# Reordered ends of a one-core attention and feed-forward kernel: queue order of the first transfers, place of the last heads' sum, and products of zeros

## The reference

```
x = x + layernorm(attention(layernorm(x)))          # 8 heads of 64, causal, sinusoidal position added to q and k
x = x + layernorm(tanh(layernorm(x) @ W1 @ W2 @ W3 + bias))
```

## Time and profile before

| | us |
|---|---|
| median of three runs | 561.74 |
| lowest and highest | 560.62 and 562.1 |
| the profiled execution | 561.25 |
| its span | 559.4 |

### The profile page before, as it was taken

The page is one execution under the profiler, slowest core; times in us unless marked ns, Lnnn a source line. Parts: engine busy times, 40 slices in busy tenths (PEclk is TensorE's granted clock), DMA queues, the critical chain, the costliest instruction groups (busy, mean ns, idle before and its releaser), DMA issues.

```text
span 559.4 us, 16795 instructions
## 1 busy us (share of the span) xinstructions
PE 537.3 (96%) x4595; PEld 455.6 (81%) x4595; DVE 469.5 (84%) x2063; ACT 409.4 (73%) x1507; POOL 398.9 (71%) x650
## 2 busy tenths in 40 slices
PE   7799999999999999999999999999999999999971
PEld 4588888888888888888888888888888888888850
DVE  4987898888889888888888888988888888888843
ACT  2777877778778777777877877777787787777740
POOL 3535777877777787777787777778777777776653
PEclk9999999999999999999999999999999999999985
DMA  5000011100000100000100010011000011100000
GB/s 160 29 2 21 11 30 30 30 19 28 20 18 28 28 28 19 28 17 21 28 28 25 22 28 9 28 28 28 19 28 24 14 28 28 28 9 21 21 9 19
DMA packets 27963, 14.53 MB, mean 26 GB/s; under 512 B 1700, under 2 KB 27431, under 8 KB 27943
## 3 DMA queue, kind: packets, MB, share of 16 engines
q1 hardware_dynamic: 27510, 13.51, 8.5%
q10 hardware_dynamic: 432, 0.79, 0.4%
HBM read 10.09 MB, written 4.19 MB: 26 GB/s over the span
## 4 chain that ended last, share of the span: by engine, by line
PE 92%; DVE 3%; ACT 2%; issue 1%; DMA 1%; POOL 1%; POOLq 0%; DVEq 0%; ACTq 0%
PE scores L879 18%; PE turned_and_heads L933 17%; PE misc_bank L994 11%; PE qk_bank L894 6%; PE qk_bank L896 5%; PE qk_bank L895 5%; PE turned_probs L910 5%; PE turned_probs L911 5%; PE turned_and_heads L919 5%; PE misc_bank L865 4%; PE misc_bank L977 3%; PE misc_bank L867 3%; PE misc_bank L866 3%; PE misc_bank L939 2%; PE misc_bank L975 1%
## 5 line engine op out<-in xcount | busy, mean ns | idle before, releaser
L263 ACT ACTIVATE probs<-scores,neg_max 128x256 f32<-128x256 f32 (+1 forms) x512 | 208.6, 425 | 43.4 <-DVE neg_max L631 43.3
L631 DVE CUSTOM_DVE_ANT_0 scores<-scores,mask 128x256 f32<-128x256 f32 (+1 forms) x512 | 166.2, 386 | 11.4 <-PE scores L879 11.4
L641 DVE TENSOR_TENSOR qk<-qk_bank,pe 128x512 f32<-128x512 f32 x128 | 87.4, 683 | 32.9 <-PE qk_bank L896 25.1
L421 POOL TENSOR_TENSOR probs<-probs,inv_sum 128x512 f32<-128x512 f32 x126 | 101.3, 823 | 12.6 <-DVE inv_sum L647 12.6
L879 PE MATMUL scores<-qk 64*128 64x256 f32 (+1 forms) x1024 | 106.6, 342 | 1.6 <-DVE qk L641 1.0
L263 ACT ACTIVATION_READ_ACCUMULATOR probs<-scores,neg_max 128x1 f32 x512 | 107.5, 210 | 0.0
L879 PEld LDWEIGHTS scores<-qk 64*128 64x128 f32 x1024 | 87.9, 186 | 18.7 <-issue 11.2
L933 PE MATMUL turned_and_heads<-pt,vals 128*64 128x256 f32 (+1 forms) x1024 | 98.5, 335 | 1.4 <-ACT pt L283 1.4
L933 PEld LDWEIGHTS turned_and_heads<-pt,vals 128*64 128x64 f32 x1024 | 64.6, 137 | 27.7 <-issue 2.0
L894 PE MATMUL qk_bank<-xt_hi,w_hi 128*128 128x256 f32 x256 | 80.5, 314 | 2.0 <-DVE qk L641 1.2
L281 ACT COPY pt<-turned_probs 128x512 f32<-128x512 f32 x128 | 76.4, 597 | 7.3 <-PE turned_probs L911 3.7
(11 more groups left out here) (91 smaller groups left out, 1013.8 us busy)
## 6 DMA issues: line engine op xcount, KB each, us to landing
x_in<-in_x SPq DMA_DIRECT2D x32, 128.0 KB, 2.2
x_res<-in_x SPq DMA_DIRECT2D x32, 128.0 KB, 2.1
out_x<-x SPq DMA_DIRECT2D x32, 128.0 KB, 1.8
w_raw<-in_w_qkv_t ACTq DMA_DIRECT2D x3, 256.0 KB, 3.8
pe<-pe_table SPq DMA_DIRECT2D x1, 256.0 KB, 5.2
wo<-in_w_o_t SPq DMA_DIRECT2D x1, 256.0 KB, 3.8
mask<-causal_mask SPq DMA_DIRECT2D x1, 128.0 KB, 5.3
w_sb<-in_w SPq DMA_DIRECT2D x2, 64.0 KB, 3.3
```

What stands on the lines that cost most here:

```text
L263: ins = nc.scalar.activation(probs[k][j][:, h, lo:hi], s_bank[j][:, h, lo:hi], ACT.Exp, bias=neg_max[k][j][:, i:i + 1], scale=-1.0, accum_ ...
L421: ins = nc.gpsimd.tensor_tensor(some, some, inv, ALU.mult)
L631: ins = nc.vector.tensor_tensor_reduce(some, some, mask[:, t * P:2 * P], -1.0, HIGHEST, ALU.add, ALU.min, neg_max[k][j][:, i:i + 1])
L641: nc.vector.tensor_tensor(qk[j][:, :], qk_bank[:, :], pe[:, :], ALU.add).then_inc(qk_kept, 1)
```

## The change

It has four parts. (1) SP issues thirds 0 and 1 of `w_raw` directly behind x 0; ACT first waits for two small memsets, runs an Exp on a 128x2 tile (with which the table load comes), and then issues third 2, `mask` and `wo`. POOL makes `half_power` and `eps` ahead of `warm`. (2) The last batch's heads are summed in `qk_bank`, by a function of its own, ahead of the feed-forward of the batch before; the DVE's instructions that read it are turned to that bank, and one wait in `turn_y` goes. (3) Zero products are added at three places of the end: 4 of 256 columns ahead of `make_heads(last, 0)`, 17 of 512 columns ahead of `turn_y(last)`, 4 of 256 columns ahead of `make_ffn(last)`. (4) The first run of zero products has 10 instead of 12. The order of DVE's, ACT's and POOL's instructions at the end is not edited.

```diff
             load(first, x_in, x_loaded)
+            for i in range(2):
+                part = slice(i * F, (i + 1) * F)
+                sp.dma_start(w_raw[:, part], w_qkv_t[:, part]).then_inc(w_in[i], 16)
             sp.dma_start(ident[:, :], ident_dram).then_inc(ident_in, 16)
             sp.dma_start(pe[:, :], pe_dram).then_inc(pe_in, 16)
-            sp.dma_start(mask[:, :], mask_dram).then_inc(mask_in, 16)
             load(first.plus(1), x_in, x_loaded)
...
-            sp.dma_start(wo[:, :, :], w_o_t.rearrange("(c f) e -> f c e", f=P)).then_inc(wo_in, 16)
...
-            for i in range(3):
-                part = slice(i * F, (i + 1) * F)
-                act.dma_start(w_raw[:, part], w_qkv_t[:, part]).then_inc(w_in[i], 16)
+
+            act.wait_ge(zeros_set, 2)
+            nc.scalar.activation(touched[:, :], eps[:, :], ACT.Exp)
+            act.dma_start(w_raw[:, 2 * F:3 * F], w_qkv_t[:, 2 * F:3 * F]).then_inc(w_in[2], 16)
+            act.dma_start(mask[:, :], mask_dram).then_inc(mask_in, 16)
+            act.dma_start(wo[:, :, :], w_o_t.rearrange("(c f) e -> f c e", f=P)).then_inc(wo_in, 16)
...
-            nc.gpsimd.memset(warm[:, :], 0.0).then_inc(warm_set, 1)
             nc.gpsimd.memset(half_power[:, :], -0.5).then_inc(zeros_set, 1)
             nc.gpsimd.memset(eps[:, :], EPS).then_inc(zeros_set, 1)
+            nc.gpsimd.memset(warm[:, :], 0.0).then_inc(warm_set, 1)
...
-                take_stats("attn", last, misc_bank[:, 0:T].rearrange("p (t e) -> p t e", t=TT))
+                take_stats("attn", last, qk_bank[:, 0:T].rearrange("p (t e) -> p t e", t=TT))
...
-                        pe_eng.wait_ge(norms["attn"]["normed"], B)
...
+            def make_attn_last():
+
+                pe_eng.wait_ge(heads_kept[0], B)
+                pe_eng.wait_ge(heads_kept[1], B)
+                pe_eng.wait_ge(qk_kept, 4 * B)
+                for t in range(TT):
+                    for p in range(PAIRS):
+                        ins = mm(qk_bank[:, t * E:(t + 1) * E], heads_t[1][:, p, t * P:(t + 1) * P], wo[:, p, :],
+                                 start=(p == 0), stop=(p == PAIRS - 1))
+                ins.then_inc(attn_made, 1)
...
-            def warm_up(n, columns=512):
+            def warm_up(n, bank, columns=512):
...
-                warm_up(12)
+                warm_up(10, qk_bank)
                 pe_eng.wait_ge(ident_in, 16)
                 turn_x(first)
-                warm_up(3, 256)
+                warm_up(3, qk_bank, 256)
...
+                warm_up(4, qk_bank, 256)
                 make_heads(last, 0)
...
                 make_heads(last, 1)
+                make_attn_last()
                 make_ffn(last.plus(-1))
-                make_attn(last, 0)
-                make_attn(last, 1)
+                pe_eng.wait_ge(exps_done, 4 * B)
+                warm_up(17, s_bank[0][:, 0, :])
                 turn_y(last)
+                warm_up(4, s_bank[0][:, 0, :], 256)
                 make_ffn(last)
```

More of the change, by code:

```diff
@@ L112, in build_block @@
         warm = sb("warm", [P, 512], BF16)
-        half_power, eps = sb("half_power", [P, TT]), sb("eps", [P, TT])
+        half_power, eps, touched = (sb(n, [P, TT]) for n in ("half_power", "eps", "touched"))
         def two(name, shape, dt=F32):
@@ L748, in norm_attn_last @@
                 for t in range(TT):
-                    ins = nc.vector.scalar_tensor_tensor(attn_n[1][:, t, :], misc_bank[:, t * E:(t + 1) * E], n["moments"][:, t, 0:1],
+                    ins = nc.vector.scalar_tensor_tensor(attn_n[1][:, t, :], qk_bank[:, t * E:(t + 1) * E], n["moments"][:, t, 0:1],
                                                          n["rstd"][:, t:t + 1].to_broadcast([P, E]), ALU.subtract, ALU.mult)
@@ L1020, in slot @@
                     make_heads(b, 0)
-            def warm_up(n, columns=512):
+            def warm_up(n, bank, columns=512):
                 for _ in range(n):
-                    mm(qk_bank[:, 0:columns], warm[:, 0:P], warm[:, 0:columns], start=True, stop=True)
+                    mm(bank[:, 0:columns], warm[:, 0:P], warm[:, 0:columns], start=True, stop=True)
             def fuse(n, lhs, rhs):
```

## The result

| | us |
|---|---|
| before, median of six | 561.59 |
| changed, median of six (562.81 to 564.9) | 564.5 |
| ratio, 95% interval | 1.0050 (1.0032 to 1.0067) |
| profiled execution and its span | 563.37, 561.6 |

The forecast was 560.9 us, the range 559.3 to 563.0. The time lies outside it, on the side of the fourth rival. The medians of the changed kernel in three later jobs were 563.9, 563.3 and 564.0, against 561.6, 561.5 and 561.3 of before.

What follows compares the result with a forecast made beforehand. PE, busy 96% of the span, bounds the middle; only the beginning and the last 25.4 us can move. Terms -0.74 - 0.28 + 1.03 - 0.82 = -0.81 us give 560.9 us, range 559.3 to 563.0.

Steps and rivals of the forecast that it cites:

- the fourth rival: Start: array still at 1.2 GHz when the first real products start; +3.6 us on the forecast, 564.5 us; chance 0.10.
- The beginning: Start of kernel: x 0 lands 1.14 us earlier, less 0.4 for a late x 1; -0.74 us.
- The turning is wanted at 5.85: Start, on PE: the turning of x is wanted at 5.85 us, after ten zero products ending near 5.35.
- Thirds 0 and 1 ... should be there by about 4 and 5. Covered: Start, SP's queue: weight thirds 0 and 1 arrive by about 4 and 5 us, wanted at 5.7; no loss.
- near 2.4 us: Start, ACT's queue: third 2 goes out near 2.4 us behind the table load, lands at 6.2, wanted about 6.6.
- the weak spot: Start, sixth place in SP's queue: x 1 may land late, losing 0 to 0.75 us; 0.4 taken.
- Ten end near 5.35 ... No cost, if the clock is up by then: Start, on PE: ten zero products instead of twelve end near 5.35 us, at no cost if the clock is up.
- keeps its length: Middle of kernel: the gain at the beginning shifts everything behind it, and the middle's length does not change.
- The order at the end: End, part 2: the sum runs earlier, but DVE's stats_ffn waits for tanh ahead of the last attn statistics; +1.03 us.
- The middle of the end: End, part 3: four zero products keep the clock up for the last batch's first heads' product; -0.28 us.
- The tail: End, part 3: seventeen zero products keep the clock up for the last turning and feed-forward; -0.82 us.
- the last clock falls: End: clock falls before the last turning, +0.15 instead of -0.82; sum +0.16, 561.9 us; chance 0.24.

Runs made afterwards that it cites:

- job 2: Changed kernel unedited, run again beside its variants on one chip, against before: 563.91 us, ratio 1.0043.
- two later jobs: Changed kernel unedited, run again twice against before: 563.91 us and 564.00 us, ratio 1.0043 in both.
- the two fillings: Changed kernel with 14 zero products at the start instead of 10: 562.02 us; with 5 of 512 columns instead of 3 of 256 behind the turning: 562.22 us.
- the order that was possible: Changed kernel with DVE's stats_ffn moved behind the last batch's attn statistics and moments: 561.85 us, beside 563.26 for the changed kernel.
- job 4's: Changed kernel without the four zero products ahead of the last batch's first heads' product: 563.46 us, ratio 1.0035 against before.
- The halves of job 1: Before's beginning with the changed end: 561.95 us, ratio 1.0009; the changed beginning with before's end: 562.84 us, ratio 1.0015, both against before.
- the one filled behind the turning alone: Changed kernel with 5 zero products of 512 columns instead of 3 of 256 between turning and first q/k product: 562.22 us, ratio 1.0017 against before.

## Why the prediction was wrong

**The beginning (-0.74, measured +2.7 in the first trace; in the medians +1.2 alone, and about +1.9 if the changed end's ratio, 1.0009, is taken from the whole's 1.0043 of two later jobs).** This is the step that failed, at three places.

The first is the identity, which has no term in the forecast. "The turning is wanted at 5.85" takes its other operand as there. Part 1 moved its transfer from second to fourth place on SP's queue, issued at 2.21 instead of 1.24; it took 4.77 us, and the turning stood at 7.03, 1.2 us late: nearly all of the 1.31 us by which x came earlier. With the identity second again the turning started at 5.88, as forecast.

The second is the thirds, which came next. "Thirds 0 and 1 ... should be there by about 4 and 5. Covered": in the first trace ACT took third 0 at 5.14 and third 1 at 5.96, waiting for both; in job 2 the same kernel took them at 4.88 and 6.41. They were wanted at about 5.1 and 5.7, so that in the first trace they cost little behind the identity; with the identity early, third 1, taken at 7.01, held the first product. I had reasoned that third 2 goes out "near 2.4 us", behind the table load in ACT's list, and the load behind the wait for two memsets. The load began at 0.73, before they were over, and the row shows the issue at 0.91, 0.18 us into the load: what sends a transfer does not wait for the arithmetic ahead of it. Third 2 thus ran beside thirds 0 and 1 on another queue, and x 1, which I had for the weak spot, was not waited for (8.25 on DVE, right behind `xt_lo`). The landing of x itself was forecast at 3.14 and was 3.00. Taking third 2, `mask` and `wo` off the other queue, with the identity in their place, gave back 1.3 us. The sizes behind x 1 were also compared unlike: 448 KB leaves out x 0 and 960 has it (448 to 832 is like with like). It had no effect.

The drain of 1.38 us that the Trainium skill ("ScalarE: Activation LUTs", section "What ACT_TABLE_LOAD costs") gives behind a table load does not appear here: the load ends at 2.01 and the Exp starts at 2.03. Nor would it have held the transfer, which went out at 0.91.

The third is "Ten end near 5.35 ... No cost, if the clock is up by then": the condition was where the cost lay. The ten ended at 5.83 (4.45 us, where I had scaled the twelve's 4.82 to 4.0), the turning waited until 7.03, and PE idled 1.20 us ahead of it and 0.69 us before the first q/k product. The granted clock was 0.50 from about 9.4 to 12.7 us and again from 19.6 to 22.9: 1.17 us lost by `row_max`, and 2.42 behind the second stretch (the copy of the values at 28.34 against 25.92). The other 0.3 us of the 2.72 came slowly over the 500 us of the middle, of which the prediction says that it "keeps its length". The rival "the array is still at 1.2 GHz" named the place and, by luck of size, the time (564.5): its price was 3.6 us, and up to `row_max` the changed kernel's four profiles lost 0.7 to 2.3 against the 5.25 at full clock. Its reason was right in some executions and not in others. In the first trace the six q/k products ran at full rate, 0.12 us apart, so the clock had risen and fell again; in job 2's changed kernel everything up to 13 us ran at half rate (256 columns 0.21 us apart). I gave it 0.10 because I priced the gaps as if the transfers came in time. That these stretches are what costs is shown by the two fillings, -2.0 and -1.8 us in one job, where in the profiles the first q/k product started 0.14 us earlier with the one (8.58 against 8.72) and 0.8 later with the other (9.52).

**The order at the end (+1.03, measured +0.88).** Right in kind and nearly in size: the sum started 0.72 us behind the heads as forecast; the feed-forward and `ffn_stats` overlapped a little more. Against the order that was possible it is 1.41 us.

**The middle of the end (-0.28, measured -0.80 in one pair of traces).** The heads' product did take 1.52 us, but in the two profiles without the four products (job 4's, and the changed beginning alone) it did so too. From its start to DVE's copy of it was 2.34 us instead of 2.69, 0.35 of the 0.80, and the scaling that follows on DVE took 1.02 us instead of 1.43. Which neighbour made it long before is open.

**The tail (-0.82, measured -0.66 in the first trace, near 0 in the median).** "Whether it stands through 2.9 us here is nearly even" looks right by the turning alone (five of eleven), but only one of eleven profiles, the first, kept the clock through most of the feed-forward (1.77 us from turning to tanh; the next is 2.05). The median of the eleven is 2.50 us from turning to tanh, against 2.44 before, so the rival "the last clock falls" is the rule here and the -0.82 the exception. The cost of the four products at half clock is seen too: 2.44 us without them, 2.65 with them. The forecast counted the rarer case as the likeliest.

**The unknown part.** The halves of job 1 add up to 1.5 us by medians and 1.3 by ratios, against 2.1 to 2.8 for the whole by its ratios. Job and chip may move the landing times; this was not pursued.

## What to carry to other kernels

A wait moved off one engine must be looked for in the order of the reader's list: the sum ran earlier, and the engine that reads it stood at an instruction that the same move had made late. When a chain starts with transfers, list every transfer that the chain reads, the small ones too, with what is in flight beside it and when each is needed; here a transfer that was wanted last, sent at once on a second queue, went with later landings of those wanted first. Zero products are worth what the gaps behind them leave: fill PE up to the product that counts, and shorten the wait in front before adding more.

## What the runs showed that was not expected

An issue on ACT's queue went out at 0.91 us while its table load ran from 0.73 to 2.01. The granted clock reads 1.00 in the first microseconds of a trace even where 512 columns take 0.43 us (ten in 4.45 us): until its first recorded change the column says nothing, and the spacing of the products has to be read instead. In job 2's changed kernel it read 1.00 from 9 to 14 us while 256 columns took 0.21 us. Gaps of 1.1 to 2.6 us of PE near the start went with half clock on the products that follow in twelve profiles, the one filled behind the turning alone among them; one, with 1.30 us, kept full clock. Behind the dense products of the end a gap of 2.8 us left the clock up through most of the feed-forward in one of eleven profiles, a gap of 1.4 us in four of four.
